# A five-layer graph network: the second edge bias is placed in PSUM by ScalarE ahead of the matmuls, and a group's window sums are added earlier in VectorE's step

## The chip, the cores and the metric

The kernel runs on one core of one Trainium2 chip. The metric is the device time of one execution in microseconds (us). TensorE is called PE in the profile, VectorE DVE, ScalarE ACT, GpSimd POOL and SyncE SP. PEld is PE's weight load, which overlaps its matmuls.

## The reference

There are 12,500 nodes with 64 features, 200,000 edges sorted by destination, 32 attributes per edge, and five layers:

```python
for l in range(5):
    h = _leaky(x @ W1[l] + b1[l]) @ W2[l] + b2[l]
    e = _leaky(edge_attr @ We1[l] + be1[l]) @ We2[l] + be2[l]
    msg = h[src] * e * dot_scale[l]
    agg = jax.ops.segment_sum(msg, dst, num_segments=n)
    out = x + agg * res_w[l]
    x = layernorm(out) * ln_g[l] + ln_b[l]
```

Before the layers the nodes are normalized and clipped at zero, and after them the input is added. The change is about `+ be2[l]`: in the kernel W2 and be2 of the edges are multiplied by `dot_scale * res_w` once per layer, which gives the tiles `w2s` and `b2s`.

## The kernel before

**Two kinds of edges.** After a preparation (until about 1230 us) each layer runs one schedule of *steps* (`edge_steps`). Edges with a destination in a dense region lie in *slot groups*: 126 per layer (`NB`), 9 chunks of 14, 1024 places each. Their h rows are made on PE by a one-hot matmul (`gathered`, L1053) from a table that SyncE loads. All other edges are in 97 *groups* of 1024 per layer and one group of spilled edges (98, `GA`). Their h rows are fetched by GpSimd with 8 indirect DMAs per group (L793) into a ring of 9 (`RING_SLOTS`). Steps 0 to 125 of a layer each handle a slot group. 92 of them handle a group too, in the pattern group, group, group, none, with a shorter run now and then, so 34 steps have none; six steps behind them (the tail) handle a group alone.

**The pipeline of one step s.** Every engine has its own unrolled program `step(s, part)`. In step s they do this:

- PE: `hidden_of` (L976) for the group and the slot group of step s+2; `edge_out` (L980) for those of step s+1, four matmuls of 128 columns each, into `e_ps` and `slot_ps` (one PSUM bank each); `window_sums` (L1016) of the group of step s; `chunk_sums` (L1029) of slot group s; `gathered` (L1053), which writes the h rows of slot group s+1 over `slot_ps`. A hidden matmul of a group waits until the windows of the steps before are added, since `win_ps` and `hid_ps[0]` share a bank.
- ACT: `hidden_tenth` (L1241) for both kinds of step s+2, a tenth of the hidden values.
- DVE: the message of the group of step s (L1750: fetched rows times `e_ps`); the message of slot group s (L1757: `slot_e` times `slot_ps`); `one_hot` for the next group (L1670, 128x640); `edge_leaky` (L1662) for both kinds of step s+2; `edge_biased` (L1666) for both of step s+1, which adds `b2s`: from `slot_ps` to the SBUF tile `slot_e`, and in place for `e_ps`; `one_hot` for slot group s+1 (L1670, up to 128x2880, its width falls from chunk to chunk: 360, 328, 288, 248, 208, 168, 128, 88, 48 columns per 128 edges); `window_added` (L1718, two adds per group); at the end of a chunk `chunk_added` (L1731).

So there is one `e_ps` and one `slot_ps`. The order within an engine is the program's; between engines semaphores are counted. The message of the group frees `e_ps` for the next `edge_out`.

**Node tiles.** When all sums of a tile of 896 nodes are in, its normalization, and in layers 0 to 3 the MLP that makes the next layer's h, is spread over six steps (of every nine, from step 18 on: 12 tiles in the loop, two in the tail). `part("middle")` and `part("end")` in a step call these pieces. In sub-step 0 PE centers, ACT squares (L1185); 1: variance, root (L1190); 2: reciprocal (L1604, in the middle) and product (L1609, at the end) on DVE; 3: affine on ACT (L1275, L1277), then at the end the first half of the MLP's first layer on PE (L845) and its bias on ACT (L1196); 4: the second half in the middle, leaky on DVE (L1599) at the end; 5: the second layer (L860) in the middle, h's bias on DVE (L1632) and the store. The last layer has no MLP. The 54 other steps of the loop are called plain here.

The bias as it is added before:

```python
def edge_biased(out, of):
    return dve.tensor_tensor(out.rearrange("p (t f) -> p t f", f=D), of.rearrange("p (t f) -> p t f", f=D),
                             b2s[:, :].unsqueeze(1).to_broadcast((P, TPG, D)), ALU.add)
```

## Time and profile before

| what | value |
|---|---|
| median of 3 runs | 6618.61 us (6609.32 to 6630.04) |
| the profiled execution's own time | 6615.82 us |
| its span, first to last instruction | 6614.0 us |
| granted PE clock, mean | 0.880 |
| instructions | 169076 |

Times below are from the start of the profiled span. A row of the timeline gives start, duration, engine, line, operation, what is written and read, and the number of merged records. A line's busy time divided by its count is the mean of one; consecutive instructions of an engine overlap by some 0.08 us, so the distance of two starts is a little under the duration. A matmul of 32-bit numbers leaves two records: `x16` at L980 is eight matmuls. "idle before" is time in which the engine had nothing, and the arrow names whom it waited for.

### The profile page before, as it was taken

To read this page: it belongs to the slowest core of one execution; us is meant where nothing else is said; L and a number is where in the kernel's file an instruction comes from. 1 tells how busy PE (TensorE), PEld (TensorE's weight loads), DVE (VectorE), ACT (ScalarE), POOL (GpSimd) and SP (SyncE) were. 2 spreads that over 40 slices of the span, in tenths; PEclk is the share of its full clock that TensorE was granted. 3 is DMA by queue.
4 is the path that set the end of the run, shared out by engine and by line. 5 is a ranking of instruction groups with operands and counts; after the bars stand their busy time and mean duration, and the time that the engine had idled before them with its cause. 6 is when DMAs were issued, how large, how long until landed. Compare 5 with 4: busy or idle time off the path is not lost.

```text
span 6614.0 us, 169076 instructions
## 1 busy us (share of the span) xinstructions
PE 5622.6 (85%) x63332; PEld 3676.7 (56%) x63333; DVE 5148.4 (78%) x7991; ACT 1133.9 (17%) x1726; POOL 4527.2 (68%) x4793
## 2 busy tenths in 40 slices
PE   6776899988888788888878888888898887888887
PEld 2223444456666555666655666655566665556665
DVE  8997544688887688888768888867888875888886
ACT  0000211111122211112211112221111222111111
POOL 5777777666677377777727777746777773777775
PEclk9997555799999799999979999988999997999998
DMA  3112399755566355656635655644565563666664
GB/s 135 26 26 47 78 240 242 185 131 138 138 148 152 96 132 136 142 141 154 159 80 133 145 143 143 162 112 116 129 147 142 148 161 78 139 147 156 151 171 110
DMA packets 733545, 886.20 MB, mean 134 GB/s; under 512 B 325488, under 2 KB 502976, under 8 KB 731568
## 3 DMA queue, kind: packets, MB, share of 16 engines
q1 hardware_dynamic: 568480, 703.64, 40.8%
q0 software_dynamic: 152144, 154.93, 12.4%
q10 hardware_dynamic: 12096, 16.53, 0.8%
q8 instruction: 530, 8.68, 0.6%
q14 instruction: 295, 2.42, 0.1%
HBM read 749.51 MB, written 125.06 MB: 132 GB/s over the span
## 4 chain that ended last, share of the span: by engine, by line
PE 54%; DVE 21%; issue 15%; DVEq 4%; ACT 3%; DMA 1%; POOL 0%; ACTq 0%; SPq 0%; POOLq 0%
PE bank L980 14%; PE bank L976 8%; PE bank L1029 7%; PE bank L1053 5%; PE bank L922 4%; PE bank L879 3%; DVE arena L1662 3%; PE bank L1016 3%; PE bank L860 2%; PE bank L845 2%; DVEq L1782 2%; DVE arena L1750 2%; ACT arena L1241 2%; DVE arena L1670 2%; DVE arena L1408 2%
## 5 line engine op out<-in xcount | busy, mean ns | idle before, releaser
L793 POOL DMA_INDIRECT arena<-h_rows,src x3855 | 3674.3, 953 | 1693.5 <-issue 1250.7
L980 PEld LDWEIGHTS bank<-w2s,arena 128*128 128x128 f32 x8960 | 1175.7, 210 | 772.3 <-DVE arena L1750 437.2
L980 PE MATMUL bank<-w2s,arena 128*128 128x128 f32 x8960 | 1307.0, 303 | 208.2 <-DVE arena L1750 191.4
L780 POOL DMA_INDIRECT slots<-arena,slot_index x792 | 787.2, 994 | 267.2 <-issue 241.3
L976 PE MATMUL bank<-nodes_state,edge_w 64*128 64x512 f32 x980 | 598.4, 693 | 307.3 <-DVE nodes_state L1718 142.6
L1053 PEld LDWEIGHTS bank<-arena 112*64 112x64 f32 x20160 | 640.4, 138 | 267.0 <-issue 245.1
L1053 PE MATMUL bank<-arena 112*64 112x64 f32 x20160 | 725.8, 225 | 60.1 <-issue 54.2
L976 PE MATMUL bank<-x_packed,edge_w 64*128 64x512 f32 x1260 | 740.1, 669 | 16.4 <-ACT std L1190 15.6
L1241 ACT ACTIVATE arena<-bank,tenth 128x512 f32<-128x512 f32 x490 | 335.5, 685 | 2296.6 <-PE bank L976 2296.6
L1662 DVE SCALAR_TENSOR_TENSOR arena<-bank,edge_w,arena 128x512 f32<-128x512 f32 x490 | 366.7, 748 | 424.1 <-ACT arena L1241 421.4
L1670 DVE TENSOR_TENSOR x_packed<-bank,slot_rel 128x2880 f32<-128x2880 f32 (+8 forms) x315 | 588.9, 1870 | 15.8 <-issue 15.8
L1670 DVE TENSOR_TENSOR arena<-bank,slot_rel 128x2880 f32<-128x2880 f32 (+8 forms) x315 | 588.6, 1869 | 12.5 <-issue 12.5
L1666 DVE TENSOR_TENSOR arena<-bank,b2s 128x512 f32<-128x512 f32 x630 | 432.4, 686 | 157.4 <-PE bank L980 153.7
L1241 ACT ACTIVATE x_packed<-bank,tenth 128x512 f32<-128x512 f32 x630 | 430.0, 683 | 680.0 <-PE bank L976 680.0
L1029 PE MATMUL bank<-x_packed,arena 64*64 64x288 f32 (+8 forms) x10080 | 524.3, 346 | 0.0
L1029 PE MATMUL bank<-arena 64*64 64x288 f32 (+8 forms) x10080 | 523.9, 346 | 0.0
L1662 DVE SCALAR_TENSOR_TENSOR arena<-bank,edge_w,x_packed 128x512 f32<-128x512 f32 x630 | 467.6, 742 | 59.5 <-ACT x_packed L1241 51.7
L1757 DVE TENSOR_TENSOR arena<-arena,bank 128x512 f32<-128x512 f32 x630 | 429.4, 682 | 43.8 <-PE bank L1053 39.1
L1016 PE MATMUL bank<-arena 128*64 128x80 f32 x7760 | 411.3, 253 | 42.4 <-DVE arena L1662 35.4
L1016 PEld LDWEIGHTS bank<-arena 128*64 128x64 f32 x7760 | 328.4, 148 | 122.3 <-DVE arena L1662 60.4
L1670 DVE TENSOR_TENSOR arena<-bank,rel 128x640 f32<-128x640 f32 x485 | 396.1, 817 | 0.0
L1029 PEld LDWEIGHTS bank<-x_packed,arena 64*64 64x64 f32 x10080 | 311.1, 135 | 127.8 <-issue 6.5
(198 smaller groups left out, 5615.6 us busy)
## 6 DMA issues: line engine op xcount, KB each, us to landing
arena<-slot_pick SPq DMA_DIRECT2D x630, 448.0 KB
arena<-h_rows SPq DMA_DIRECT2D x630, 224.0 KB
x_packed<-slot_attr SPq DMA_DIRECT2D x630, 128.0 KB
nodes_state<-attr_t SPq DMA_DIRECT2D x485, 128.0 KB
arena<-h_rows,src POOLq DMA_INDIRECT x3855
slot_pick<-arena SPq DMA_DIRECT2D x126, 448.0 KB
x_packed<-slots SPq DMA_DIRECT2D x127, 136.0 KB, 4.9
slots<-arena SPq DMA_DIRECT2D x9, 1904.0 KB, 22.1
```

The source lines that it names most:

```text
L780: pool.indirect_dma_start(slots, bass.IndirectOffsetOnAxis(ap=slot_index[:, t:t + 1], axis=0), records[:, v, j, :], None).then_inc(record_ ...
L793: pool.indirect_dma_start(to[0:n, at:at + D], None, table, bass.IndirectOffsetOnAxis(ap=index[0:n, t:t + 1], axis=0)).then_inc(landed(t), 16)
L976: return pe.matmul(hid_ps[k][:, :], edge_w[rows_of, 0:P], attributes, start=True, stop=True)
L980: mm = pe.matmul(to[:, j * P:(j + 1) * P], acts[:, j * TILE:(j + 1) * TILE], w2s[:, :], start=True, stop=True)
L1016: mm = pe.matmul(win_ps[side * D:(side + 1) * D, 0:WIN], msg[:, 0, at:at + D], pick[:, k % 2, side * TPH + j, :], start=(j == 0), stop=(j ...
L1029: mm = pe.matmul(sum_ps[half][side * D:(side + 1) * D, 0:w], msg[slots_of, 1, at:at + D], slot_places[i % 2][slots_of, k * w:(k + 1) * w], ...
L1053: mm = pe.matmul(slot_ps[half * D:(half + 1) * D, k * D:(k + 1) * D], source_pick[0:ROWS, i % 2, slot:slot + D], source_rows[0:ROWS, i % 2 ...
L1241: return act.activation(hid_tenth[k], hid_ps[k][:, :], ACT.Identity, scale=SLOPE, bias=tenth[:, :])
L1662: return dve.scalar_tensor_tensor(out, hid_ps[k][:, :], edge_w[:, 2 * P + D:2 * P + D + 1], hid_tenth[k], ALU.add, ALU.max)
L1666: return dve.tensor_tensor(out.rearrange("p (t f) -> p t f", f=D), of.rearrange("p (t f) -> p t f", f=D), b2s[:, :].unsqueeze(1).to_broadc ...
L1670: return dve.tensor_tensor(out, column_ps[:, 0:n].unsqueeze(1).to_broadcast((P, tiles, n)), where.unsqueeze(2).to_broadcast((P, tiles, n)) ...
L1757: dve.tensor_tensor(msg[:, 1, :], slot_e, slot_ps[:, :], ALU.mult).then_inc(slot_msg_ready, 1)
```

## The change

ScalarE writes the bias `b2s` into the whole bank (`bias(e_ps)`, `bias(slot_ps)`), and the matmuls of `edge_out` add onto it (`start=False`) where they overwrote before. For `e_ps` nothing more is done. For `slot_ps` ScalarE copies the finished e to `slot_e`, since `gathered` overwrites the bank. VectorE's `edge_biased` is left only in the far pass. So that a matmul adds, each layer opens with eight matmuls over the two banks, and the first of the `gathered` matmuls in each half alone has `start=True`. `window_added` moves from behind the `one_hot` of the next slot group to before the node part "middle".

```diff
-            def edge_out(acts, to):
+            def edge_out(acts, to, onto_bias):
                 for j in range(TPH):
                     mm = pe.matmul(to[:, j * P:(j + 1) * P], acts[:, j * TILE:(j + 1) * TILE],
-                                   w2s[:, :], start=True, stop=True)
+                                   w2s[:, :], start=not onto_bias, stop=True, skip_group_check=onto_bias)
...
+                for to in (e_ps, slot_ps):
+                    for j in range(TPH):
+                        mm = pe.matmul(to[:, j * P:(j + 1) * P], ident[:, :], ones[:, :], start=(j == 0), stop=True,
+                                       skip_group_check=True)
+                mm.then_inc(banks_written, 1)
...
-                    if now == SPILL_AT:
-                        pe.wait_ge(spill_msg_ready, l + 1)
-                    elif now is not None:
-                        pe.wait_ge(msg_ready, l * GR + real(now) + 1)
                     if m is not None:
                         pe.wait_ge(hid_acted[0], l * GA + m + 1)
-                        edge_out(hidden[:, 0, m % 2, :], e_ps).then_inc(e_ready, 1)
+                        pe.wait_ge(e_begun, l * GA + m + 1)
+                        edge_out(hidden[:, 0, m % 2, :], e_ps, True).then_inc(e_ready, 1)
...
+                        pe.wait_ge(slot_e_begun, l * NB + k + 1)
...
+                def bias(to):
+                    return act.activation(to[:, :].rearrange("p (t f) -> p t f", f=D),
+                                          b2s[:, :].unsqueeze(1).to_broadcast((P, TPG, D)), ACT.Identity)
+
                 def step(s, part):
+                    now, m = a_at(s), a_at(s + 1)
+                    if now == SPILL_AT:
+                        act.wait_ge(spill_msg_ready, l + 1)
+                    elif now is not None:
+                        act.wait_ge(msg_ready, l * GR + real(now) + 1)
+                    if m is not None:
+                        bias(e_ps).then_inc(e_begun, 1)
...
+                    if i is not None:
+                        act.wait_ge(slot_msg_ready, l * NB + i + 1)
+                    i = b_at(s + 1)
+                    if i is not None:
+                        bias(slot_ps).then_inc(slot_e_begun, 1)
...
                     for side, n, k in ((0, GA, a_at(s + 2)), (1, NB, b_at(s + 2))):
                         if k is not None:
                             act.wait_ge(hid_ready[side], l * n + k + 1)
                             hidden_tenth(side).then_inc(tenth_ready[side], 1)
+                    if i is not None:
+                        act.wait_ge(slot_e_ready, l * NB + i + 1)
+                        act.activation(slot_e, slot_ps[:, :], ACT.Identity).then_inc(slot_e_kept, 1)
                     part("middle")
...
-                    if i is not None:
-                        dve.wait_ge(slot_e_ready, l * NB + i + 1)
-                        edge_biased(slot_e, slot_ps[:, :]).then_inc(slot_e_biased, 1)
-                    if m is not None:
-                        dve.wait_ge(e_ready, l * GA + m + 1)
-                        edge_biased(e_ps[:, :], e_ps[:, :]).then_inc(e_biased, 1)
+                    if k is not None and k != SPILL_AT:
...
+                        window_added(s, k)
                     part("middle")
```

**Where the rows move.** DVE, a plain step of the first chunk with a group (step 9; L1782 before and L1795 after read the window's start). Before:

```order
L1750 TENSOR_TENSOR arena<-arena,bank 128x512 [waits rows_landed4,e_biased]
...
L1757 TENSOR_TENSOR arena<-arena,bank 128x512 [waits sum_ready]
L1670 TENSOR_TENSOR arena<-bank,rel 128x640
...
L1662 SCALAR_TENSOR_TENSOR arena<-bank,edge_w,x_packed 128x512 [waits tenth_ready1]
L1666 TENSOR_TENSOR arena<-bank,b2s 128x512 [waits slot_e_ready]
L1666 TENSOR_TENSOR bank<-bank,b2s 128x512 [waits e_ready]
L1670 TENSOR_TENSOR arena<-bank,slot_rel 128x2880
...
L1716 REGISTER_ALU [waits win_ready]
L1718 ISA [waits added]
L1718 TENSOR_TENSOR nodes_state<-nodes_state,bank 64x80
```

After:

```order
L1778 TENSOR_TENSOR arena<-arena,bank 128x512 [waits rows_landed4,e_ready]
...
L1785 TENSOR_TENSOR arena<-arena,bank 128x512 [waits sum_ready]
L1698 TENSOR_TENSOR arena<-bank,rel 128x640
...
L1690 SCALAR_TENSOR_TENSOR arena<-bank,edge_w,x_packed 128x512 [waits tenth_ready1]
...
L1744 REGISTER_ALU [waits win_ready]
L1746 ISA [waits added]
L1746 TENSOR_TENSOR nodes_state<-nodes_state,bank 64x80
...
L1698 TENSOR_TENSOR arena<-bank,slot_rel 128x2880
```

The two L1666 are gone, and the wait for `win_ready` with its two adds now stands ahead of the long `one_hot`.

ACT, from sub-step 3 of a node tile to the start of sub-step 5 (L1275 and L1303 are the affine, L1196 and L1199 the MLP's bias, L1241 and L1244 the tenth). Before:

```order
L1275 ACTIVATE nodes_state<-normed,ln_w 64x448
...
L1277 ACTIVATE nodes_state<-normed,ln_w 64x448
...
L1196 ACTIVATE y_sum<-bank,node_w 128x112x4 [waits y_ready]
...
L1241 ACTIVATE arena<-bank,tenth 128x512 [waits hid_ready0]
...
L1241 ACTIVATE x_packed<-bank,tenth 128x512 [waits hid_ready1]
...
L1196 ACTIVATE y_sum<-bank,node_w 128x112x4 [waits y_ready]
```

After:

```order
L1303 ACTIVATE nodes_state<-normed,ln_w 64x448
...
L1305 ACTIVATE nodes_state<-normed,ln_w 64x448
...
L1199 ACTIVATE y_sum<-bank,node_w 128x112x4 [waits y_ready]
...
L1258 ACTIVATE bank<-b2s 128x512
L1258 ACTIVATE bank<-b2s 128x512 [waits slot_msg_ready]
...
L1244 ACTIVATE arena<-bank,tenth 128x512 [waits hid_ready0]
...
L1244 ACTIVATE x_packed<-bank,tenth 128x512 [waits hid_ready1]
L1285 ACTIVATE arena<-bank 128x512 [waits slot_e_ready]
...
L1199 ACTIVATE y_sum<-bank,node_w 128x112x4 [waits y_ready]
```

The two bias writes (L1258) stand behind the MLP's bias of the step before and ahead of the tenths, the copy (L1285) behind them.

PE, the matmuls of `edge_out` (L980 in both) in a plain step of the first chunk. Before:

```order
L980 MATMUL bank<-w2s,arena 128x128 [waits hid_acted0,msg_ready]
L980 MATMUL bank<-w2s,arena 128x128 x3
L980 MATMUL bank<-w2s,arena 128x128 [waits hid_acted1,slot_msg_ready]
L980 MATMUL bank<-w2s,arena 128x128 x3
```

After:

```order
L980 MATMUL bank<-w2s,arena 128x128 [waits e_begun,hid_acted0]
L980 MATMUL bank<-w2s,arena 128x128 x3
L980 MATMUL bank<-w2s,arena 128x128 [waits slot_e_begun,hid_acted1]
L980 MATMUL bank<-w2s,arena 128x128 x3
```

PE waits for the bias write where it waited for the message; the message is waited for by ACT.

## Rows read from the trace of the kernel before

**Rows 1.** The page, part 1: busy time, share and instructions of each engine.
```profile
PE 5622.6 (85%) x63332; PEld 3676.7 (56%) x63333; DVE 5148.4 (78%) x7991; ACT 1133.9 (17%) x1726; POOL 4527.2 (68%) x4793
```

**Rows 2.** The page, part 4: the chain that ended last, by engine.
```profile
PE 54%; DVE 21%; issue 15%; DVEq 4%; ACT 3%; DMA 1%; POOL 0%; ACTq 0%; SPq 0%; POOLq 0%
```

**Rows 3.** Groups by line and shape: busy, mean ns; idle before, releasers.
```profile
L1666 DVE TENSOR_TENSOR arena<-bank,b2s 128x512 f32<-128x512 f32 x630 | 432.4, 686 | 157.4 <-PE bank L980 153.7 <-issue 0.2
L1666 DVE TENSOR_TENSOR bank<-bank,b2s 128x512 f32<-128x512 f32 x490 | 337.7, 689 | 37.8 <-PE bank L980 37.8
L1210 ACT ACTIVATE arena<-bank 98x512 f32<-98x512 f32 x126 | 75.2, 597 | 374.4 <-PE bank L901 330.7 <-DMA slot_attr<-arena 43.7
L1241 ACT ACTIVATE arena<-bank,tenth 128x512 f32<-128x512 f32 x490 | 335.5, 685 | 2296.6 <-PE bank L976 2296.6
L1185 ACT ACTIVATE square<-bank 128x448 f32<-128x448 f32 x79 | 43.0, 544 | 1130.5 <-PE bank L954 676.7 <-PE bank L833 453.8
L793 POOL DMA_INDIRECT arena<-h_rows,src x3855 | 3674.3, 953 | 1693.5 <-issue 1250.7 <-DMA h_rows<-piece_rows 299.3 <-DMA src<-src_tiles 143.4
```

**Rows 4.** The tile w2s: duration min/median/max, first and last start of its matmuls.
```profile
L980 PE MATMUL bank<-w2s,arena x8960: 274/275/583, 1239.4 to 6592.1; 128*128 128x128 f32 x200
```

**Rows 5.** Timeline, all engines, step 9 of layer 1 (plain, with a group).
```profile
2409.52 0.67 DVE L1750 TENSOR_TENSOR arena<-arena,bank 128x512 f32<-128x512 f32 x1
...
2410.32 2.05 PE L980 MATMUL bank<-w2s,arena 128*128 128x128 f32 x16 [0.81 <-DVE arena L1750]
...
2412.30 0.77 PE L1016 MATMUL bank<-arena 128*64 128x80 f32 x16
...
2413.00 2.65 PE L1029 MATMUL bank<-x_packed,arena 64*64 64x360 f32 x32
...
2413.61 3.15 DVE L1670 TENSOR_TENSOR arena<-bank,slot_rel 128x2880 f32<-128x2880 f32 x1
...
2415.58 1.15 PE L1053 MATMUL bank<-arena 112*64 112x64 f32 x32
...
2416.68 0.59 DVE L1718 TENSOR_TENSOR nodes_state<-nodes_state,bank 64x80 f32 x2
...
2417.30 0.69 DVE L1750 TENSOR_TENSOR arena<-arena,bank 128x512 f32<-128x512 f32 x1
```

**Rows 6.** DVE timeline, the next two steps: with a group, and without.
```profile
2424.97 0.69 DVE L1757 TENSOR_TENSOR arena<-arena,bank 128x512 f32<-128x512 f32 x1
2425.57 0.82 DVE L1670 TENSOR_TENSOR arena<-bank,rel 128x640 f32<-128x640 f32 x1
2427.03 0.75 DVE L1662 SCALAR_TENSOR_TENSOR arena<-bank,edge_w,arena 128x512 f32<-128x512 f32 x1 [0.64 <-ACT arena L1241]
2427.70 0.74 DVE L1662 SCALAR_TENSOR_TENSOR arena<-bank,edge_w,x_packed 128x512 f32<-128x512 f32 x1
...
2432.70 0.67 DVE L1750 TENSOR_TENSOR arena<-arena,bank 128x512 f32<-128x512 f32 x1
```

**Rows 7.** ACT timeline of a node tile, layer 2: sub-steps 1, 3, 4, 5.
```profile
3581.84 0.54 ACT L1185 ACTIVATE square<-bank 128x448 f32<-128x448 f32 x1 [6.51 <-PE bank L833]
3582.29 0.68 ACT L1241 ACTIVATE arena<-bank,tenth 128x512 f32<-128x512 f32 x1
...
3613.52 1.02 ACT L1196 ACTIVATE y_sum<-bank,node_w 128x448 f32<-128x448 f32 x1 [7.29 <-PE bank L845]
...
3621.75 0.69 ACT L1241 ACTIVATE x_packed<-bank,tenth 128x512 f32<-128x512 f32 x1 [1.03 <-PE bank L976]
```

**Rows 8.** PE timeline of the same tile.
```profile
3602.41 0.66 PE L976 MATMUL bank<-nodes_state,edge_w 64*128 64x512 f32 x1 [3.52 <-DVE nodes_state L1718]
...
3604.23 2.04 PE L980 MATMUL bank<-w2s,arena 128*128 128x128 f32 x8 [0.59 <-issue]
...
3614.21 2.05 PE L980 MATMUL bank<-w2s,arena 128*128 128x128 f32 x16
...
3620.59 1.12 PE L976 MATMUL bank<-x_packed,edge_w 64*128 64x512 f32 x2
3622.23 2.05 PE L980 MATMUL bank<-w2s,arena 128*128 128x128 f32 x16 [0.52 <-DVE arena L1750]
```

**Rows 9.** DVE timeline of the same tile: sub-steps 2, 3, 5.
```profile
3595.98 2.94 DVE L1604 RECIPROCAL rstd<-std 128x448 f32<-128x448 f32 x1
...
3603.44 0.68 DVE L1757 TENSOR_TENSOR arena<-arena,bank 128x512 f32<-128x512 f32 x1
...
3621.42 0.68 DVE L1750 TENSOR_TENSOR arena<-arena,bank 128x512 f32<-128x512 f32 x1
```

38 lines of the change are left out of this document (21 added, 17 removed).

## The prediction

> **What bounds the kernel now.** I read the page's busy times first. PE is busy for 85% of the span and DVE for 78%, ACT for 17% and POOL for 68% [rows 1]. No engine is full, so the step's loop between PE and DVE has to be read. The chain that ended last says the same: 54% PE, 21% DVE, 15% issue, and ACT 3% [rows 2]. The change takes work from the second and gives work to an engine that stands in the chain for 3%. The groups by line give what is taken: 630 and 490 adds of the bias, 686 and 689 ns each [rows 3], 770 us of DVE's busy time. That is no forecast, since what matters is which wait ends last in a step.
>
> So I read the timeline of one plain step in the widest chunk. DVE's message of the group starts at 2409.52 and the next one at 2417.30, 7.78 us later, and DVE has hardly a gap between. PE waits 0.81 us for the message, then works through L980, L1016, L1029 and L1053 [rows 5]. The long `one_hot` on DVE runs while PE does its window sums, chunk sums and gather. This overlap is what the change touches: the adds of the window now stand ahead of that `one_hot`, and they need PE's window sums of the same step.
>
> POOL is a floor and not the bound. Its 3855 fetches take 953 ns each plus 0.32 us of issue (1250.7 over 3855) [rows 3], 1.28 us, so a layer of 771 fetches cannot be under some 985 us, and five of them not under 4930. The first L980 of the layers starts at 1239.4 and the last at 6592.1 [rows 4], 5353 us: some 420 us could be saved before POOL stops it.
>
> **The new operations.** No row shows a bias write by ACT. The nearest is L1210, ACT's plain copy from PSUM of 512 columns, 597 ns [rows 3]; above lies the 512-column operation with a per-partition bias, 685, below the 448-column square, 544. I take 0.60 us, since neither the write nor the copy has a bias column, and keep 0.54 and 0.69. The Trainium skill speaks against the move: "ScalarE: Activation LUTs", Rules for kernel authors, wants adds on VectorE and not on ScalarE. The trace here has a DVE add at 0.69 and an ACT pass at 0.60 [rows 3], so I don't follow it; by the rule the ACT pass is at least as dear as DVE's, and with 0.69 in each of 126 steps of five layers the sum below is 57 us higher.
>
> **Term 1, plain steps with a group.** New loop, from message to message: message 0.69, hand-over 0.05, bias write 0.60, hand-over 0.05, the eight matmuls of L980 1.98 (2412.30 less 2410.32), window sums 0.77, hand-over 0.05, two adds with their gap 0.62 (2417.30 less 2416.68), `one_hot` 3.07 (2416.68 less 2413.61) [rows 5]: 7.88. A hand-over is read off a pair: PE's L976 ends at 3621.71 and ACT starts at 3621.75 [rows 7, 8]. The second bias write waits for the slot message, 0.60 behind the first message, and so is done before PE needs it. PE's own work in the step is 1.1 for L976 [rows 8], 1.98, 0.70, 2.58 and, for L1053, 1.1 [rows 5], 7.5 in all, so the chain decides. Before, the step took 7.78 and the next 7.67 (2424.97 less 2417.30) [rows 5, 6]. The change loses 0.10 and 0.21; with full steps of 8 us elsewhere I take 0.12 lost on average. DVE gives up 1.2 us of adds and gets a wait for ACT and PE of about that length.
>
> **Term 2, plain steps without a group.** Before: 2424.97 to 2432.70, 7.73 [rows 6]. Here no message of a group holds up the first bias write and no window is added. New on DVE: slot message 0.69, bias write 0.65 with its hand-over, tenth 0.69 [rows 3], two `edge_leaky` 1.41, `one_hot` 3.07: 6.5. PE needs 1.1 + 1.98 + 2.58 + 1.1, 6.7, and decides. Saved 1.03. In four steps, three with a group and one without, that is 0.36 lost and 1.03 won, 0.17 us per step. The bounds are 0 and 0.35, the latter if DVE's wait for the window vanishes. 54 plain steps per layer: 9 us won.
>
> **Term 3, node tiles.** ACT now has its new work in line with the tile's. Sub-step 1: before, the tenth ran right behind the square, at 3582.29 [rows 7]; now two bias writes stand between, 1.2 us, of which PE's own L980 covers about 0.5: 0.7 lost. Sub-step 2: DVE goes into the reciprocal (3595.98, 2.94 us [rows 9]) with two adds of 0.60 less ahead of it, and nothing else is waited for: 1.2 won. Sub-step 3: PE starts L980 at 3604.23, right behind the slot message that ends at 3604.12 [rows 8, 9]; now a bias write stands between: 0.6 lost. Sub-step 4: the MLP's bias on ACT runs from 3613.52 to 3614.54 [rows 7] and PE starts L980 at 3614.21 without waiting for it [rows 8]; now the bias write of `e_ps` is behind it, ready at 3615.2: 1.0 lost. Sub-step 5: the message ends at 3622.10 and PE starts at 3622.23 [rows 8, 9]; now 3622.80: 0.6 lost. Together 0.7 - 1.2 + 0.6 + 1.0 + 0.6, 1.7 us per tile. Bounds: 0, if other waits cover it, and 3, if each delay is also met by DVE. 12 tiles per layer: 20.4 us lost in layers 0 to 3. In layer 4, without MLP, 0.1 per tile: 1 us.
>
> **Term 4, tail and opening.** In the tail no long `one_hot` runs. DVE's work per step was 0.60 + 0.74 + 0.67 + 0.60 + 0.62 (message, `one_hot`, `edge_leaky`, bias, adds by their distances [rows 5, 6]), 3.2; the new loop is 0.69 + 0.05 + 0.60 + 0.05 + 0.99 + 0.77 + 0.05 + 0.62, 3.8: six steps, 3.6 us lost. The eight opening matmuls cost at most the 2.05 of eight others [rows 5]; they run while the first fetches of the layer are under way, which is the cover; I take 1 us per layer, 10 in all if it is gone.
>
> The adds moved ahead of the reciprocal also free PE's next L976, which waited 3.52 us at 3602.41 [rows 8]. I cost this at nothing: behind it PE waits for the message anyway, which comes from DVE after the same reciprocal and `one_hot`. POOL's ring and SP's loads hang on the messages, whose pace hardly changes.
>
> **Sum.** Layers 0 to 3: -9 + 20.4 + 3.6 + 1 = +16 each. Layer 4: -9 + 1 + 3.6 + 1 = -3.4. Together +61 us on the profiled execution's own 6615.8: 6677. The median of the runs lies 2.8 above that execution, so I forecast 6680.
>
> **The rivals.**
> A. *DVE's relief arrives.* If PE's and ACT's delays in the tile steps fall into waits that are there anyway (PE idles 15% of the span), term 3 is nothing and all 126 steps win 0.17: 107 us, less term 4's 23: 6535. For it: DVE has hardly a gap in [rows 6], and 770 us leave it. Against it: the long `one_hot` no longer runs beside PE's window sums. It decides if PE starts L980 in sub-steps 4 and 5 less than 0.3 us later behind what it waits for than before. 6500 to 6595, chance 0.26.
> B. *PE's clock.* After the 3.52 us without work PE ran at the lower of its levels, 1.2 GHz: eight records of L980 took 2.04 at 3604.23 and sixteen 2.05 at 3614.21 [rows 8]. In the new order PE does L976 early and then idles through the reciprocal, `one_hot`, the message and the bias write, longer than before in chunks with a narrow `one_hot`. If four more tiles of a layer are met by it at 3 us each (half of the step's 6 us of matmuls again), that is 60 us more: 6740. The Trainium skill, "TensorE: Matmul & The Clock Gate", What's actually happening, says that the array's clock follows how busy it was lately; the rows agree. Chance 0.12, 6740 to 6800.
> C. *It cancels.* Terms 1 and 2 at their better bound (-19 us a layer) against term 3 and 4 as worked: within 20 us of 6619. Chance 0.12.
> That the work does not move is excluded, since the order of the new program has the L1666 rows gone.
>
> **Chances and range.** The forecast's case, 6640 to 6740, has 0.50, with B's 0.12 slower; A is faster; 0.3%, 20 us, is about what a measurement of this kernel can tell from no change, and C lies within it. So: faster 0.26, same 0.12, slower 0.62. The range reaches into A until about 0.1 is left below, 6535, and up to 6800, which takes in the tile bound of 3 us with ACT's 0.69 in part.
>
> **What would show it.** In the new profile DVE's busy time should fall by some 770 us, ACT's should rise by 1750 passes of 0.60, 1050 us. A plain step with a group in the first chunk should take 7.9 us, one without 6.7. A wait of DVE's adds for PE's window sums should stand among the long ones, about 1 us a step, and PE's L980 should wait for ACT where it waited for L1750. Per tile six steps should be 1.7 us longer. I am wrong if ACT's bias write is under 0.5 us, if tile steps are not longer, or if PE's idle time falls.

## The result, and the profile after

The changed kernel takes 6687.14 us, the median of 5 runs (6670.81 to 6701.93), against 6619.8 for the kernel before (5 runs, 6609.32 to 6630.04): a ratio of 1.0104, 95% interval 1.0082 to 1.0127. On a second chip it was 1.0094 (1.0071 to 1.0118). The forecast was 6680.

The profiled execution is the slowest of the five, 6701.93 us, with a span of 6700.2 and a mean granted clock of 0.885 (before: 0.880). The page of the changed kernel, part 1 (busy time by engine), and from part 4 (the chain that ended last, by engine) the first line:

```profile
PE 5592.7 (83%) x63412; PEld 3667.1 (55%) x63413; DVE 4515.5 (67%) x6871; ACT 2101.7 (31%) x3476; POOL 4524.2 (68%) x4793
...
PE 43%; issue 16%; DVE 16%; POOL 12%; ACT 8%; DVEq 3%; DMA 1%; ACTq 0%; SPq 0%; POOLq 0%
```

Against [rows 1], DVE is busy for 633 us less and ACT for 968 more. Neither says anything of the time, which rose. In the chain ACT has gone from 3% to 8% [rows 2].

The groups by line and shape of the changed kernel: `L1258` is the bias write, `L1285` the copy of the slot group's e, `L1746` the adds of the window, `L1690` the leaky of a group's hidden values. Further on `L1778` is the message of the group, `L1785` that of the slot group, `L1022` the window sums and `L1698` the `one_hot`.

```profile
L1258 ACT ACTIVATE bank<-b2s 128x512 f32<-128x512 f32 x1120 | 666.3, 603 | 1957.7 <-DVE arena L1785 1156.4 <-DVE arena L1778 768.2 <-DVE x_packed L1774 19.4
L1285 ACT ACTIVATE arena<-bank 128x512 f32<-128x512 f32 x630 | 376.4, 597 | 428.9 <-PE bank L980 404.8 <-issue 1.5
L1746 DVE TENSOR_TENSOR nodes_state<-nodes_state,bank 64x80 f32 x970 | 228.0, 235 | 676.3 <-PE bank L1022 578.0 <-issue 34.1
...
L1690 DVE SCALAR_TENSOR_TENSOR arena<-bank,edge_w,arena 128x512 f32<-128x512 f32 x490 | 367.8, 751 | 623.3 <-ACT arena L1244 622.8 <-issue 0.5
```

Three of the changed kernel's longest waits (engine and line, whom they waited for: us in total, times, longest us):

```profile
DVE arena L1690 <- ACT arena L1244: 622.8, 489, 8.9
DVE nodes_state L1746 <- PE bank L1022: 578.0, 453, 8.2
PE bank L980 <- ACT bank L1258: 494.2, 408, 4.9
```

Three waits have taken the place of the adds that left. DVE waits 578 us for PE's window sums, where the same adds (L1718) waited for PE for 1.6 us in all in the kernel before, by its group:

```profile
L1718 DVE TENSOR_TENSOR nodes_state<-nodes_state,bank 64x80 f32 x970 | 223.2, 230 | 129.1 <-issue 62.9 <-PE bank L1016 1.6
```

PE waits 494 us for the bias write, 408 times. And DVE's wait for the tenth grew from 421.4 to 622.8 us.

The timeline of the changed kernel, step 9 of layer 1, the step of [rows 5]. A row gives start, duration, engine and line, and in brackets the idle time ahead of it:

```profile
2420.42 0.68 DVE L1778 TENSOR_TENSOR arena<-arena,bank 128x512 f32<-128x512 f32 x1
...
2421.14 1.20 ACT L1258 ACTIVATE bank<-b2s 128x512 f32<-128x512 f32 x2 [3.53 <-DVE arena L1778]
...
2421.88 2.02 PE L980 MATMUL bank<-w2s,arena 128*128 128x128 f32 x16 [0.20 <-ACT bank L1258]
...
2422.97 0.75 DVE L1690 SCALAR_TENSOR_TENSOR arena<-bank,edge_w,x_packed 128x512 f32<-128x512 f32 x1 [0.54 <-ACT x_packed L1244]
2423.83 0.78 PE L1022 MATMUL bank<-arena 128*64 128x80 f32 x16
...
2424.87 0.60 DVE L1746 TENSOR_TENSOR nodes_state<-nodes_state,bank 64x80 f32 x2 [1.14 <-PE bank L1022]
2425.50 3.16 DVE L1698 TENSOR_TENSOR arena<-bank,slot_rel 128x2880 f32<-128x2880 f32 x1
...
2428.57 0.68 DVE L1778 TENSOR_TENSOR arena<-arena,bank 128x512 f32<-128x512 f32 x1
```

The new loop stands here link by link: message 0.68, ACT begins 0.04 behind it, first write 0.60, PE begins 0.14 behind that, L980 1.95, window sums 0.78, DVE's adds 0.26 behind their end, 0.63, `one_hot` 3.07 to the next message. That is 8.15 us where it was 7.78.

**A table by kind of step.** From the trace I took, for each step, the distance from its first message on DVE to the next step's, and summed these over the steps of a layer (the message of the spilled group is not counted as one). It is the mean of layers 0 to 3 unless it says layer 4. The two last columns are variants that the next section tells of; their kernels and the changed kernel of the third column were profiled on the same chip.

| us per layer | before | changed, first chip | changed, second chip | slot part alone | slot part, adds late |
|---|---|---|---|---|---|
| 36 plain steps with a group | 250.6 | 271.6 | 271.3 | 264.7 | 253.0 |
| 14 plain steps without | 96.0 | 75.7 | 75.8 | 84.8 | 85.2 |
| 72 tile steps | 609.9 | 633.7 | 624.1 | 618.8 | 611.5 |
| 72 tile steps, layer 4 | 571.5 | 575.7 | 572.1 | 577.8 | 558.0 |

The four steps at the ends of chunks stay within 2 us of 29. The tail, from the last slot message to the last message of a group, is 54.0 to 60.2 us before and 52.4 to 62.2 after. The two executions of the changed kernel differ by 10 us a layer in the tile steps and by nothing in the plain ones, so a difference of a few us in the tile row is no finding.

**Outside the steps.** The first message on DVE came at 1246.8 us in the kernel before and at 1231.1 and 1234.4 in the two executions of the changed one, and in the other variants between 1234.9 and 1245.0. The preparation is the same code in all of them, so this is a difference between executions, of up to 16 us. From the first message to the end the changed kernel took 101.9 us more than the kernel before on the first chip and 58.7 on the second.

### The profile page after: what moved, and what is told of

Same layout as the page of the kernel before. It is cut to its first block, busy times and chain, and to the rows that moved or that the text cites. A ratio compares the mean times of both kernels' runs of the same rounds, so it can differ in the third digit from the quotient of the medians.

```text
span 6700.2 us, 171519 instructions
## 1 busy us (share of the span) xinstructions
PE 5592.7 (83%) x63412; PEld 3667.1 (55%) x63413; DVE 4515.5 (67%) x6871; ACT 2101.7 (31%) x3476; POOL 4524.2 (68%) x4793
## 3 DMA queue, kind: packets, MB, share of 16 engines
q8 instruction: 535, 8.77, 0.6%
## 4 chain that ended last, share of the span: by engine, by line
PE 43%; issue 16%; DVE 16%; POOL 12%; ACT 8%; DVEq 3%; DMA 1%; ACTq 0%; SPq 0%; POOLq 0%
PE bank L980 12%; POOL slots L780 11%; PE bank L1035 9%; PE bank L1059 5%; PE bank L1022 5%; PE bank L976 4%; ACT bank L1258 3%; DVE arena L1698 3%; ACT arena L1244 3%; DVE arena L1778 3%; DVE arena L1690 2%; DVE x_packed L1698 2%; DVE arena L1785 2%; PE bank L845 2%; PE bank L860 2%
## 5 line engine op out<-in xcount | busy, mean ns | idle before, releaser
L980 PEld LDWEIGHTS bank<-w2s,arena 128*128 128x128 f32 x8960 | 1165.4, 208 | 1051.8 <-issue 1050.9
L980 PE MATMUL bank<-w2s,arena 128*128 128x128 f32 x8960 | 1295.1, 301 | 498.1 <-ACT bank L1258 494.2
L1258 ACT ACTIVATE bank<-b2s 128x512 f32<-128x512 f32 x1120 | 666.3, 603 | 1957.7 <-DVE arena L1785 1156.4
L1690 DVE SCALAR_TENSOR_TENSOR arena<-bank,edge_w,arena 128x512 f32<-128x512 f32 x490 | 367.8, 751 | 623.3 <-ACT arena L1244 622.8
L976 PE MATMUL bank<-x_packed,edge_w 64*128 64x512 f32 x1260 | 718.4, 651 | 16.0 <-ACT std L1193 16.0
L1746 DVE TENSOR_TENSOR nodes_state<-nodes_state,bank 64x80 f32 x970 | 228.0, 235 | 676.3 <-PE bank L1022 578.0
L976 PE MATMUL bank<-nodes_state,edge_w 64*128 64x512 f32 x980 | 579.2, 673 | 117.1 <-ACT std L1193 53.0
L1698 DVE TENSOR_TENSOR arena<-bank,slot_rel 128x2880 f32<-128x2880 f32 (+8 forms) x315 | 592.2, 1880 | 52.9 <-issue 46.6
L1698 DVE TENSOR_TENSOR x_packed<-bank,slot_rel 128x2880 f32<-128x2880 f32 (+8 forms) x315 | 591.9, 1879 | 53.2 <-issue 47.2
L1690 DVE SCALAR_TENSOR_TENSOR arena<-bank,edge_w,x_packed 128x512 f32<-128x512 f32 x630 | 468.9, 744 | 144.0 <-ACT x_packed L1244 144.0
L1035 PE MATMUL bank<-arena 64*64 64x288 f32 (+8 forms) x10080 | 547.6, 358 | 0.0
L1285 ACT ACTIVATE arena<-bank 128x512 f32<-128x512 f32 x630 | 376.4, 597 | 428.9 <-PE bank L980 404.8
L1785 DVE TENSOR_TENSOR arena<-arena,bank 128x512 f32<-128x512 f32 x630 | 428.9, 681 | 59.9 <-PE bank L1059 56.4
L1022 PE MATMUL bank<-arena 128*64 128x80 f32 x7760 | 419.2, 256 | 34.6 <-DVE arena L1690 29.1
L1244 ACT ACTIVATE x_packed<-bank,tenth 128x512 f32<-128x512 f32 x630 | 426.5, 677 | 8.8 <-PE bank L976 8.5
L1022 PEld LDWEIGHTS bank<-arena 128*64 128x64 f32 x7760 | 336.3, 151 | 115.4 <-DVE arena L1690 43.5
L1035 PEld LDWEIGHTS bank<-arena 64*64 64x64 f32 x10080 | 323.4, 141 | 137.4 <-issue 19.3
```

Of the source, the lines that this page charges most:

```text
L976: return pe.matmul(hid_ps[k][:, :], edge_w[rows_of, 0:P], attributes, start=True, stop=True)
L980: mm = pe.matmul(to[:, j * P:(j + 1) * P], acts[:, j * TILE:(j + 1) * TILE], w2s[:, :], start=not onto_bias, stop=True, skip_group_check=o ...
L1022: mm = pe.matmul(win_ps[side * D:(side + 1) * D, 0:WIN], msg[:, 0, at:at + D], pick[:, k % 2, side * TPH + j, :], start=(j == 0), stop=(j ...
L1035: mm = pe.matmul(sum_ps[half][side * D:(side + 1) * D, 0:w], msg[slots_of, 1, at:at + D], slot_places[i % 2][slots_of, k * w:(k + 1) * w], ...
L1244: return act.activation(hid_tenth[k], hid_ps[k][:, :], ACT.Identity, scale=SLOPE, bias=tenth[:, :])
L1258: return act.activation(to[:, :].rearrange("p (t f) -> p t f", f=D), b2s[:, :].unsqueeze(1).to_broadcast((P, TPG, D)), ACT.Identity)
```

## The experiments

**Two kinds of chip time.** The first six runs and the last two were made on chips on which the kernel before itself took 11.11 to 11.26 ms, with the same program and the same data. The four in between ran beside a kernel before of 6612.36 us. What made the first slow is open; what its trace shows stands at the end of this section. These four come first, since they speak of the change as it was timed.

### The change itself on another chip, and its two halves

The slot part alone, against the changed kernel. ScalarE keeps the slot groups' bias and copy, and the group's e gets its bias from VectorE, so that PE waits for the message again:

```diff
# PE
+                    if now == SPILL_AT:
+                        pe.wait_ge(spill_msg_ready, l + 1)
+                    elif now is not None:
+                        pe.wait_ge(msg_ready, l * GR + real(now) + 1)
...
-                        pe.wait_ge(e_begun, l * GA + m + 1)
-                        edge_out(hidden[:, 0, m % 2, :], e_ps, True).then_inc(e_ready, 1)
+                        edge_out(hidden[:, 0, m % 2, :], e_ps, False).then_inc(e_ready, 1)
...
# ACT, with its waits for the group's message
-                        bias(e_ps).then_inc(e_begun, 1)
...
# DVE, behind the leakies
+                    if m is not None:
+                        dve.wait_ge(e_ready, l * GA + m + 1)
+                        edge_biased(e_ps[:, :], e_ps[:, :]).then_inc(e_biased, 1)
```

The slot part with the adds late is the same with `window_added(s, k)` behind the long `one_hot`, where it stood before. The group part alone is the other half: ScalarE writes `e_ps`, and `edge_biased(slot_e, slot_ps[:, :])` stays on VectorE.

> The changed kernel itself, beside the kernel before on the same chip as the variants below. Its ratio was 1.010 where the kernel before takes 6.62 ms; it is not known where the kernel before takes 11.2 ms. Theory H (the hand-overs through ScalarE cost what the tiles lost): 1.008 to 1.013, and the two parts taken apart below lie on both sides of it. Rival O (where the adds stand on VectorE costs it): the change lies at the 1.011 that was measured with the adds late or above it, since the adds late should then have helped.

> ScalarE writes the bias of the slot groups alone and copies their e; the group's e gets its bias from VectorE as before, so TensorE's edge_out for a group starts on the message directly; the adds stand early. Theory H: the costly hand-over (message, ScalarE's write, matmuls) is gone for a group while VectorE is still relieved of 0.69 us in 126 steps of a layer: ratio 0.990 to 1.000, and a node tile's sub-steps 3 to 5 are as before. Rival O: the adds are where they are in the change, so nothing changes against the change itself: within 0.3% of it.

> The same, and the adds behind the long one_hot as before. Theory H: as the slot part with the adds early, within 0.5% of it, 0.990 to 1.002. Rival O: 0.5% or more below the slot part with the adds early. If ScalarE's copy of the slot e comes late for the gather, both slot versions are slower than before.

> ScalarE writes the bias of a group's e alone; the slot groups' e gets its bias from VectorE as before; the adds early. Theory H: the costly hand-over is in, the relief is only 0.69 us in 98 steps: ratio at that of the change or above, 1.008 to 1.015. Rival: the cost lies in the slot part (its copy, its wait ahead of the tenths): 1.000 to 1.003.

| kernel | median us | runs | ratio to before | 95% interval |
|---|---|---|---|---|
| the change itself | 6671.3 | 4 | 1.0094 | 1.0071 to 1.0118 |
| slot part alone, adds early | 6654.93 | 5 | 1.0058 | 1.0040 to 1.0077 |
| slot part alone, adds late | 6557.55 | 4 | 0.9915 | 0.9898 to 0.9932 |
| group part alone, adds early | 6704.15 | 4 | 1.0131 | 1.0112 to 1.0151 |

What follows:

**In the slot part the place of the adds costs most.** Between the two slot versions nothing differs but the place of two adds of 0.6 us, and the time differs by 97 us, 6654.93 less 6557.55, or 1.5%. Theory H had wanted them within 0.5%; it falls on this point. The kernel with the adds late beats the kernel before and the change. Its ratio of 0.9915 says that ScalarE's relief is real, for the slot part, once VectorE isn't sent into a new wait. In the profiled executions it takes 58 us less than the kernel before, of which 12 lie in the preparation, which the edit doesn't touch, and 46, 0.7%, behind it. By the table this gain lies in the steps without a group (85.2 against 96.0) and in layer 4's tile steps; the plain steps with a group take 253.0, no less than the 250.6 before.

The timelines of both, step 9 of layer 1. First the slot part with the adds early (L1773 is the message, L1689 VectorE's bias add, L1741 the adds, L1693 the `one_hot`):

```profile
2421.01 0.67 DVE L1773 TENSOR_TENSOR arena<-arena,bank 128x512 f32<-128x512 f32 x1
...
2424.12 0.77 PE L1022 MATMUL bank<-arena 128*64 128x80 f32 x16
2424.22 0.69 DVE L1689 TENSOR_TENSOR bank<-bank,b2s 128x512 f32<-128x512 f32 x1
...
2425.16 0.60 DVE L1741 TENSOR_TENSOR nodes_state<-nodes_state,bank 64x80 f32 x2 [0.25 <-PE bank L1022]
...
2425.79 3.16 DVE L1693 TENSOR_TENSOR arena<-bank,slot_rel 128x2880 f32<-128x2880 f32 x1
...
2428.87 0.68 DVE L1773 TENSOR_TENSOR arena<-arena,bank 128x512 f32<-128x512 f32 x1
```

The same step with the adds late:

```profile
2381.85 0.67 DVE L1773 TENSOR_TENSOR arena<-arena,bank 128x512 f32<-128x512 f32 x1
...
2384.96 0.78 PE L1022 MATMUL bank<-arena 128*64 128x80 f32 x16
2385.06 0.69 DVE L1689 TENSOR_TENSOR bank<-bank,b2s 128x512 f32<-128x512 f32 x1
...
2385.66 3.15 DVE L1693 TENSOR_TENSOR arena<-bank,slot_rel 128x2880 f32<-128x2880 f32 x1
...
2388.72 0.59 DVE L1741 TENSOR_TENSOR nodes_state<-nodes_state,bank 64x80 f32 x2
2389.34 0.69 DVE L1773 TENSOR_TENSOR arena<-arena,bank 128x512 f32<-128x512 f32 x1
```

Up to the bias add both are alike to 0.01 us (3.21 us from message to bias add). Then the early adds wait 0.25 us for the end of the window sums and take 0.63, and the long `one_hot`, which waits for nobody, starts 4.78 us behind the message instead of 3.81. Put behind it, the adds find their sums long ready. The step takes 7.86 us against 7.49. Over a layer this is 264.7 less 253.0, 11.7 us, in the 36 plain steps with a group and nothing in the 14 without, and 7.3 in the tile steps, which is within that row's scatter (19.8 in layer 4, which is not). Behind the first message the two profiled executions differ by 97 us, as the medians do. The groups by line say where the idle time is. The adds of the slot part with the adds early:

```profile
L1741 DVE TENSOR_TENSOR nodes_state<-nodes_state,bank 64x80 f32 x970 | 228.0, 235 | 385.5 <-PE bank L1022 281.6 <-issue 31.7 <-DVE nodes_state L1741 4.3
```

The same group with the adds late, 23.6 us of waiting for PE where it was 281.6:

```profile
L1741 DVE TENSOR_TENSOR nodes_state<-nodes_state,bank 64x80 f32 x970 | 223.9, 231 | 150.1 <-issue 59.9 <-PE bank L1022 23.6 <-DVE nodes_state L1741 2.8
```

**The group part costs little more, with the adds early.** The slot part alone still lies above the kernel before, though no ScalarE write stands between message and L980 for a group. That was expected at 0.990 to 1.000 by Theory H and within 0.3% of the change by Rival O, and 1.0058 lies outside the first; against the change it is 0.36% lower by the two ratios and 0.25% by the two medians, so the second is neither met clearly nor missed. Putting the group part on top of it gives the change: 1.0094, with intervals that overlap. In the table it is a trade: 36 steps with a group lose 6.6 us (271.3 less 264.7), since the write's 0.60 and its hand-overs stand in their loop; 14 steps without one win 9.0, since no message and no `e_ps` add stands in theirs; the tile steps lose 5.3, within their scatter.

**The slot part is what relieves.** The group part alone, 1.0131, is the slowest by its median, and within Theory H's 1.008 to 1.015: a layer's 36 steps with a group take 275.9 us there. In its trace VectorE's bias add of the slot group waits 0.82 us for L980 in step 9, which a ScalarE write holds up, and the adds wait another 0.86 for the window sums. The low end of the expectation, the rival's 1.000 to 1.003, is out.

### Where ScalarE's own order costs

The slot part has a price too, which the kind of step shows. This is the mean us of a plain step over layers 0 to 3 (the change on the second chip); the three signs say whether this step, the next and the one behind it have a group (G) or none (-):

| step | count per layer | before | change | slot part, adds early | slot part, adds late | group part |
|---|---|---|---|---|---|---|
| G G G | 11 | 7.23 | 7.78 | 7.68 | 7.37 | 7.94 |
| G G - | 14 | 6.91 | 7.41 | 7.00 | 6.53 | 8.03 |
| G - G | 11 | 6.76 | 7.45 | 7.47 | 7.32 | 6.93 |
| - G G | 14 | 6.85 | 5.41 | 6.06 | 6.09 | 5.72 |

In G - G both slot versions lose 0.56 to 0.71 us, though no group's e is made there and PE's L980 works for the slot group alone. In the group part it is 0.17. The timeline of such a step, step 10 of layer 1, in the kernel before:

```profile
2417.30 0.69 DVE L1750 TENSOR_TENSOR arena<-arena,bank 128x512 f32<-128x512 f32 x1
...
2418.64 0.69 ACT L1241 ACTIVATE arena<-bank,tenth 128x512 f32<-128x512 f32 x1 [8.40 <-PE bank L976]
...
2420.17 0.77 PE L1016 MATMUL bank<-arena 128*64 128x80 f32 x16 [0.25 <-DVE arena L1662]
```

The same step in the slot part with the adds late (L1261 is its bias write, L1247 the tenth, L1022 the window sums):

```profile
2389.34 0.69 DVE L1773 TENSOR_TENSOR arena<-arena,bank 128x512 f32<-128x512 f32 x1
...
2390.66 0.60 ACT L1261 ACTIVATE bank<-b2s 128x512 f32<-128x512 f32 x1 [5.00 <-DVE arena L1780]
2391.20 0.67 ACT L1247 ACTIVATE arena<-bank,tenth 128x512 f32<-128x512 f32 x1
2391.41 1.13 PE L980 MATMUL bank<-w2s,arena 128*128 128x128 f32 x8 [0.53 <-ACT bank L1261]
...
2392.71 0.78 PE L1022 MATMUL bank<-arena 128*64 128x80 f32 x16 [0.17 <-DVE arena L1685]
...
2397.32 0.69 DVE L1780 TENSOR_TENSOR arena<-arena,bank 128x512 f32<-128x512 f32 x1 [0.43 <-PE bank L1059]
```

The window sums wait for DVE's leaky (they share a bank with the hidden values), and the leaky for the tenth. The tenth needs nothing from the slot message, but stands in ACT's queue behind the bias write, which does: it starts 1.86 us behind the group's message, not 1.34, and the window sums 3.37, not 2.87. From there on PE is the bound, and DVE waits 0.43 for its gather. The same kind of step is 4 of the 12 sub-steps 5 of the node tiles, and takes 36.8 and 37.7 us a layer in the two slot versions, 30.3 before and 30.5 with the group part alone. This is read from one timeline and from the contrast with the group part alone; no run changed ACT's order by itself. A bias write behind the tenths should not do that, but should hold up L980 for the slot group.

### The adds and ScalarE's tile work, on the slow chips

The other eight runs, of four kernels, were made for the same question. The adds early alone is the kernel before with the one block moved; the adds late is the changed kernel with it moved back:

```diff
# the block; early it stands ahead of part("middle"), late behind ends_chunk(s)'s adds
                    if k is not None and k != SPILL_AT:
                        ...
                        window_added(s, k)
```

And in ScalarE's list of tile pieces (`tile_biased_both` calls the low and the high half in turn):

```diff
-                tile_parts = {("loop", 0, "end"): lambda i: tile_squared, ("loop", 1, "end"): lambda i: tile_root,
+                tile_parts = {("loop", 1, "middle"): lambda i: tile_squared, ("loop", 1, "end"): lambda i: tile_root,
...
-("loop", 3, "end"): lambda i: tile_biased_low, ("loop", 4, "middle"): lambda i: tile_biased_high,
+("loop", 4, "middle"): lambda i: tile_biased_both,
```

> The kernel before with one edit: window_added stands before the node part, ahead of the long one_hot, as in the change. Theory (the step's loop now runs through ACT's bias write and PE before the adds): without that write PE's window sums are done some 3 us after the message while DVE reaches the adds only after its two bias adds, at some 4.9 us, so nothing waits; a plain group step of the first chunk stays at 7.7 to 7.8 us, ratio to the kernel before 0.993 to 1.001. Rival (the early place of the adds is the loss by itself, as they cut the one_hot off from PE's sums): 8.1 us in that step, ratio 1.007 to 1.012.

> The changed kernel with window_added put back behind the long one_hot. Theory: DVE then has 7.6 to 7.7 us of work and waits in a plain group step of the first chunk (message 0.6, slot message 0.6, then the tenth at 2.6, two leaky 1.4, one_hot 3.07, adds 0.62) where it took 8.15; 92 such steps per layer at 0.3 to 0.45 less are 140 to 200 us under the changed kernel, a ratio to the kernel before of 0.98 to 0.99; the wait DVE L1746 for PE L1022 (578 us) is gone. Rival (ACT in line with the messages is the loss, wherever the adds stand): PE waits the same 494 us for ACT and the ratio stays at 1.008 to 1.013.

> The changed kernel with the node tile's square moved on ACT from the end of sub-step 0 to the middle of sub-step 1, and the first MLP bias from the end of sub-step 3 to the middle of sub-step 4, so that neither stands ahead of bias writes and tenths. Theory (0.7 and 1.0 us of the 1.7 per tile come from this queue): 12 tiles in four layers win up to 1.7 us, 40 to 80 us, a ratio to the kernel before of 0.998 to 1.004. Rival (the tile steps are longer only through the adds' wait for PE, as the plain ones): no change, 1.009 to 1.012.

> Both edits of the two runs before on the changed kernel. Theory: both losses are taken away and DVE's 770 us of bias adds are a gain at last: the sum of the two gains, a ratio to the kernel before of 0.97 to 0.985. Rival (PE bounds the steps once DVE is relieved, so the second edit adds nothing): the same time as with the adds late alone.

> The changed kernel with window_added behind the long one_hot once more, in a job where the kernel before should take its usual 6.6 ms, since in the first job it took 11.2 ms and PE stood between its own instructions. Theory: 92 group steps per layer without the adds' wait for PE, 0.98 to 0.99 of the kernel before. Rival (ACT in line with the messages is the loss, wherever the adds stand): 1.008 to 1.013.

> The same with the tile's square and first MLP bias moved back on ACT, once more. Theory: 0.97 to 0.985 of the kernel before. Rival (PE bounds the steps once DVE is relieved): no different from the run with the adds late alone.

> The whole change, but the adds stand behind the long one_hot as in the kernel before; where the kernel before takes 6.6 ms. Theory O (the early adds cost some 1.4%, whatever else is done, as between the two slot versions, 1.0058 and 0.9915): 1.0094 * 0.9915 / 1.0058, so 0.992 to 0.998. Theory H (ScalarE's write between message and matmuls of a group costs, and the adds matter only with the slot part alone): 1.004 or more. The difference to the slot part with the adds late, 0.9915, is then what the group part of the bias costs with the adds late; with the adds early it was 0.36%.

> The kernel before with the adds alone moved ahead of the long one_hot; no bias is moved. Theory O: 1.010 to 1.018, with the plain steps with a group longer by 0.3 to 0.6 us in the widest chunk and DVE waiting for the window sums. Rival R (the early adds only cost since VectorE, relieved, comes to them before TensorE has the sums; with the bias adds still ahead of them the sums are ready): within 0.3% of 1.000, and no wait of DVE at the adds over 0.2 us a step.

| kernel | median us | ratio to before | 95% interval |
|---|---|---|---|
| adds early alone | 11258.76 | 1.0016 | 0.9987 to 1.0044 |
| the same, another chip | 11120.14 | 1.0020 | 1.0002 to 1.0039 |
| change, adds late | 11377.05 | 1.0110 | 1.0068 to 1.0153 |
| the same, another chip | 11375.3 | 1.0111 | 1.0068 to 1.0154 |
| the same, a third | 11228.93 | 1.0103 | 1.0077 to 1.0129 |
| change, tile work of ACT late | 11329.28 | 1.0059 | 1.0034 to 1.0085 |
| change, both late | 11279.97 | 1.0029 | 1.0004 to 1.0054 |
| the same, another chip | 11303.3 | 1.0029 | 1.0002 to 1.0057 |

The theories had expected 0.98 to 0.99 with the adds late, 0.998 to 1.004 with the tile work late, and 0.97 to 0.985 with both; none was met, and the adds late came out in the range of the rival, 1.008 to 1.013. The numbers repeat well, on three chips, and yet none of them can be carried to the 6.6 ms. The page of the adds early alone shows why: part 1, part 4's first line, and three groups.

```profile
PE 7402.3 (66%) x63332; PEld 4608.0 (41%) x63333; DVE 5239.6 (47%) x7991; ACT 1139.3 (10%) x1726; POOL 4517.1 (40%) x4793
...
PE 46%; issue 20%; another core or an unknown queue 19%; DVE 11%; ACT 2%; DVEq 2%; ACTq 0%; DMA 0%; POOL 0%; SPq 0%; POOLq 0%
...
L793 POOL DMA_INDIRECT arena<-h_rows,src x3855 | 3670.0, 952 | 5738.2 <-DMA src<-src_tiles 4044.7
L980 PE MATMUL bank<-w2s,arena 128*128 128x128 f32 x8960 | 1649.8, 348 | 1194.3 <-issue 552.0
...
L1053 PE MATMUL bank<-arena 112*64 112x64 f32 x20160 | 1151.1, 251 | 930.4 <-issue 877.9
```

DVE, ACT and POOL are busy as long as at 6.6 ms, to 2%, and one fetch of POOL takes 952 ns as before. PE alone is slower: it stands between its own matmuls for nothing that the profile shows ("issue"), 878 us at L1053. The first 15 of one gather's 32 records came in pieces of one to four, from 5006.58 on:

```profile
5006.58 0.34 PE L1053 MATMUL bank<-arena 112*64 112x64 f32 x4 [0.85 <-issue]
5007.99 0.49 PE L1053 MATMUL bank<-arena 112*64 112x64 f32 x4 [1.07 <-issue]
5008.72 0.27 PE L1053 MATMUL bank<-arena 112*64 112x64 f32 x1 [0.23 <-issue]
```

Steps of 28 us are found there, and an order of ACT and DVE that costs 0.4 us a step at 6.6 ms is lost in it. What is still of use are the shortest steps of a kind, which no such gap met. Of the steps with a group, ahead of another with one and then one without, the shortest in the widest chunk took 8.07 us in the changed kernel (at 6.6 ms) and 7.34, 7.51 and 7.53 in the three runs with the adds late; in the narrowest 5.47, and 5.08 in all three. The two slot versions differ by 0.29 and 0.35 by the same measure. These are not the same steps (5 against 12, 116 against 123), and a step that follows a gap need not be one of the steady loop, so this points the same way and shows nothing. That the whole change with the adds late beats the kernel before in a run is not shown: the run for it, expected at 0.992 to 0.998, was made on a slow chip and gave 1.0103.

What the adds early cost in the kernel before, whose VectorE comes to them later, can be read from such steps with more right, since the same step stands in both traces: step 34 takes 7.54 us in three of the five layers of the second run of the adds early alone, and 7.52 to 7.53 before; steps 15, 26 and 52 take at their shortest 7.87, 8.28 and 7.21, and 7.85, 8.26 and 7.19 before. All four are steps followed by two more with a group. Of those ahead of one with and one without, step 1 of layer 4 alone met no gap: 8.04 and 8.10 in the two runs, 8.10 before. Step 34 of layer 0, second run (L1016 are the window sums, L1666 the bias add, L1718 the adds, L1750 the messages):

```profile
2371.34 0.67 DVE L1750 TENSOR_TENSOR arena<-arena,bank 128x512 f32<-128x512 f32 x1
...
2374.06 0.77 PE L1016 MATMUL bank<-arena 128*64 128x80 f32 x16
...
2375.18 0.69 DVE L1666 TENSOR_TENSOR bank<-bank,b2s 128x512 f32<-128x512 f32 x1
2375.78 0.59 DVE L1718 TENSOR_TENSOR nodes_state<-nodes_state,bank 64x80 f32 x2
...
2378.88 0.68 DVE L1750 TENSOR_TENSOR arena<-arena,bank 128x512 f32<-128x512 f32 x1
```

The sums are done at 2374.83, and VectorE, with two bias adds ahead of its own adds, comes to them at 2375.78 and waits for nobody. So in a step that no gap met, the early place costs some 0.02 us there; in the slot part it costs 0.31 in the mean of such steps (7.68 less 7.37) and 0.37 in step 9. The ratios 1.0016 and 1.0020, against the expected 1.010 to 1.018, speak for the rival too, but of executions that PE's gaps rule. As far as these steps show, the place of the adds is not dear by itself; it becomes so when VectorE has less to do ahead of them.

The tile work of ACT late was expected to show whether ScalarE's order in the tiles matters. With the adds late it took the ratio from 1.0110 to 1.0029 on the same chip, and from 1.0111 to 1.0029 on another. This holds for that kind of execution alone. The changed kernel itself was not run on a slow chip, so the 1.0059 with the tile work late alone has nothing to stand against.

## Why the prediction was right, and where its steps were not

The forecast of 6680 lies 7 us from the median, and rival A (6500 to 6595), B (PE's clock) and C did not occur: the granted clock is 0.885 and 0.893 in the two profiles, no lower than before. Several terms were wrong against each other, though, and part of the closeness is luck. The forecast was 16 us more per layer in layers 0 to 3. From a layer's first message to the last of its tail the traces have 24.4 more on the first chip and 15.4 on the second, and in layer 4 6.6 more and 0.5 less, for a forecast of 3.4 less. And the preparation, which no term speaks of, was 12 to 16 us shorter in the two profiled executions of the change.

**Term 1** said 0.12 us lost per plain step with a group. It is 0.57: (271.3 less 250.6) over 36. The chain of links is the right one and decides the step, but the hand-overs were mis-sized. I took all three at 0.05 from a pair of PE and ACT, where [rows 8, 9] already showed 0.13 from DVE's message to PE. They measure 0.04 (DVE to ACT), 0.14 (ACT to PE) and 0.26 (PE's window sums to DVE's adds), 0.44 in place of 0.15, which is the whole way from 7.88 to 8.15. And by kind the loss is 0.50 to 0.69: in G - G, with 0.69 the dearest, it isn't this loop that decides but the late tenth, which I hadn't worked out.

**Term 2** said 1.03 us saved per plain step without a group; it is 1.44, (96.0 less 75.8) over 14. Such a step takes 6.34 us in the widest chunk, where I had 6.7 by PE's own work: in step 11 of layer 1 PE's L976 starts 0.66 us ahead of the message, in the step before. Terms 1 and 2 together were to win 9 us a layer and win nothing (+0.5).

**Term 3** said 1.7 us lost per tile, 20.4 a layer. It is 14.2 and 23.8 a layer in the two executions, 1.2 and 2.0 per tile. The size was right, but by sub-steps the attribution was in part wrong, so that the sum is in part luck. Sub-step 4, which I put at 1.0, has the mechanism that I named. The timeline of the changed kernel, same tile:

```profile
3649.06 1.02 ACT L1199 ACTIVATE y_sum<-bank,node_w 128x448 f32<-128x448 f32 x1 [3.89 <-PE bank L845]
...
3649.88 1.20 ACT L1258 ACTIVATE bank<-b2s 128x512 f32<-128x512 f32 x2
...
3650.71 2.02 PE L980 MATMUL bank<-w2s,arena 128*128 128x128 f32 x16 [0.89 <-ACT bank L1258]
```

PE is held for 0.89 us by the write that stands behind the MLP's bias. The first tile's sub-step 4 takes 9.64 us with the group part in (9.68 with it alone) and 8.77, 8.78 and 8.81 in the three kernels without it. So in this tile the 0.9 is shown from both sides. Over all 12 tiles it is not: sub-step 4 takes 100.4 us a layer before, 111.6 in the change, and 105.0, 109.5 and 105.0 in the slot part with the adds early, with the adds late, and in the group part alone. Summed over 12 tiles, per tile and by my sub-steps (second chip): sub-step 1 -0.2 (forecast +0.7), 2 -0.7 (-1.2), 3 -0.3 (+0.6), 4 +0.9 (+1.0), 5 +0.6 (+0.6, but in good part by the late tenth and not by the group's hand-over), and sub-step 0, of which the forecast said nothing, +0.8 (100.7 less 91.2 over 12). This last goes with the early adds: 100.1 and 102.7 in the two other kernels with the adds early, 93.1 with them late.

**Term 4.** The opening was to lose 1 us a layer; from the last message of a layer to the first of the next it is 41.9 to 45.2 us before and 41.4 to 44.4 after. The tail was to lose 3.6 us and shows -1.6 to +3.4, within what its own values scatter. Layer 4's tile steps lost 4.2 and 0.6, not 1.0 and within the same scatter.

**The order that was not priced.** The prediction said that the adds ahead of the reciprocal bring nothing, and said against rival A that the long `one_hot` no longer runs beside PE's window sums. Term 1's loop has that order in it, but nowhere was it set against the other one, as a part of the change with a price of its own. Between the two slot versions, which differ in it alone, it is worth 1.5%. For the change itself an estimate from the step shown above: the last leaky ends 3.30 us behind the message (2422.97 and 0.75, less 2420.42), the `one_hot` adds 3.07 and the adds 0.62, 7.0 in all, less than the 7.5 of PE's own work in Term 1. With the adds late PE would then bound the step at some 7.5 us instead of 8.15. No run at 6.6 ms shows it.

**Prices.** The bias write took 603 ns and the copy 597; 0.60 was assumed. The Trainium skill's rule for adds ("ScalarE: Activation LUTs", Rules for kernel authors) has its ground in bf16 and did not hold for the f32 pass here, 603 against DVE's 686 to 689 [rows 3]. DVE's busy time fell by 633 us and not by 770: I had multiplied by durations where consecutive passes overlap by 0.08, and 1120 adds of 0.60 make 672; the other 39 are not accounted for. In the same way ACT's 1750 passes brought 968 us and not 1050.

## What to carry to other kernels

When a change moves work to an idle engine and at the same time reorders the engine that it relieves, price the two apart, and run them apart: here the relief by the slot part was worth 0.85% and the new order cost 1.5% on top of it, while in the kernel before the same order cost some 0.02 us in the steps that could be compared. Work that needs nobody, like the long `one_hot`, belongs between the request to another engine and the use of its answer; two short adds put ahead of it brought a wait for that answer, 0.25 us in step 9 of the slot part and 1.14 in the change. And a queue that gets a waiting instruction hands that wait to all that stands behind it, here the tenths, so what needs no wait should be looked at first in the new order.

## What the runs showed of the hardware that was not expected

- Hand-overs between engines are not one number: in one step 0.04 us from DVE's message to ACT, 0.14 from ACT's write to PE's matmul, 0.26 from the modelled end of PE's sums to DVE's add.
- The same program takes 6.61 ms on some chips and 11.11 to 11.26 on others. PE's busy time was 7402 us and not 5623 there, with up to 1.07 us between two matmuls of one gather, at a mean granted clock of 0.715 against 0.880. The order of the variants was another one there. What is behind it was not found.
- ScalarE's pass took the same time into PSUM (the write, 603 ns) as out of it (the copy, 597), so where its output lies made no difference of note here. The Trainium skill ("ScalarE: Activation LUTs", ACT is a hardware spline evaluator) has PSUM as the port of lower latency for an ACTIVATE's destination; these two passes, which also differ in their source, don't show it.
